# Squares turned together with T's summands, inverse norms spread by two DMAs, x's low parts on GpSimd

## The reference, cut to what matters

```python
# x: (64, 128, 512) = 64 items, 128 rows, 512 columns; adj: (128, 128); four weights of (512, 512)
def _L0_gnn_ref(x, weight, bias):            # graph over the 512 columns
    x_norm = xn / norm(xn)                   # xn = x transposed to (512, 64, 128)
    mean_sim = einsum('nbl,mbl->nm', x_norm, x_norm) / B
    A = mean_sim on its k nearest, else 0    # k = 153, then normalised by degrees -> An
    return einsum('sd,sbl->dbl', An, xn @ weight) + bias

def _L1_gnn_ref(h, causal_mask, W_lang, W_grav, W_V, W_O, gate_logit, log_sigma):   # per item, 128 rows
    z_l, z_g, v = h @ W_lang.T, h @ W_grav.T, h @ W_V.T
    zn = z_l / norm(z_l)
    A_l = maximum(zn @ zn.T, 0) * not_eye
    sq = sum(z_g * z_g, -1)
    d2 = maximum(sq + sq.T - 2 * z_g @ z_g.T, 0)
    A_g = exp(-d2 / (2 * sigma * sigma)) * not_eye
    K = w_l * row_stochastic(A_l * mask) + (1 - w_l) * row_stochastic(A_g * mask)
    return (K @ v) @ W_O.T

x = layernorm(x + _L0_gnn_ref(x, adj, bias))
x = layernorm(x + _L1_gnn_ref(x, adj, W_lang, W_grav, W_V, W_O, gate_logit, log_sigma))
```

## Time and profile before

| | us |
|---|---|
| median of 3 runs (lowest, highest) | 947.16 (945.18, 949.78) |
| the profiled execution's own time | 945.65 |
| its span, first to last instruction | 943.9 |
| PE busy in the span | 915.0 (97%) |
| DVE busy | 750.7 (80%) |
| ACT busy | 535.5 (57%) |
| POOL busy | 307.6 (33%) |

### The profile page before, as it was taken

How to read it: one execution, slowest core, us unless ns; L and a number is a source line. 1 busy time by engine, 2 the same in 40 slices (tenths; PEclk the granted TensorE clock), 3 DMA queues, 4 the chain that set the end, 5 groups by cost and what they waited for, 6 DMA issues and landing times.

```text
span 943.9 us, 18952 instructions
## 1 busy us (share of the span) xinstructions
PE 915.0 (97%) x6858; PEld 538.8 (57%) x6858; DVE 750.7 (80%) x1716; ACT 535.5 (57%) x978; POOL 307.6 (33%) x431
## 2 busy tenths in 40 slices
PE   8999998999999999999999999999999999999993
PEld 6777876565555555555555555555555555555451
DVE  5887588778787878787878787878787878786766
ACT  6887766666463736364646464646464646463531
POOL 5888272045040505050504040404040404041410
PEclk9999999999999999999999999999999999999997
DMA  7554121103232223222323232313131313121211
GB/s 306 188 200 149 54 91 45 46 1 58 89 54 94 56 89 56 88 57 87 59 86 59 85 66 79 69 76 74 71 74 71 81 63 87 59 57 46 57 45 44
DMA packets 101848, 75.84 MB, mean 80 GB/s; under 512 B 80560, under 2 KB 80688, under 8 KB 99888
## 3 DMA queue, kind: packets, MB, share of 16 engines
q1 hardware_dynamic: 101808, 75.32, 27.7%
HBM read 38.86 MB, written 16.78 MB: 59 GB/s over the span
## 4 chain that ended last, share of the span: by engine, by line
PE 62%; DVE 14%; ACT 4%; issue 3%; DMA 1%; POOL 1%; DVEq 0%; SPq 0%; ACTq 0%; POOLq 0%
PE bank L265 13%; PE bank L267 12%; PE bank L266 12%; PE pair L265 7%; PE pair L267 7%; PE pair L266 7%; DVE arena L1731 4%; DVE arena L1724 2%; DVE arena L1399 1%; PE bank L778 1%; ACT arena L1071 1%; DMA arena<-arena 1%; ACT arena L1210 1%; PE bank L753 1%; PE bank L752 1%
## 5 line engine op out<-in xcount | busy, mean ns | idle before, releaser
L265 PE MATMUL bank<-arena 128*128 128x512 f16 (+2 forms) x1056 | 292.9, 301 | 7.4 <-DMA arena<-arena 3.1
L266 PE MATMUL bank<-arena 128*128 128x512 f16 (+2 forms) x1056 | 292.4, 301 | 0.0
L267 PE MATMUL bank<-arena 128*128 128x512 f16 (+2 forms) x1056 | 292.4, 301 | 0.0
L265 PE MATMUL pair<-arena 128*128 128x512 f16 (+1 forms) x400 | 151.1, 378 | 0.0
L266 PE MATMUL pair<-arena 128*128 128x512 f16 (+1 forms) x400 | 150.6, 377 | 0.0
L267 PE MATMUL pair<-arena 128*128 128x512 f16 (+1 forms) x400 | 150.4, 377 | 0.0
L265 PEld LDWEIGHTS bank<-arena 128*128 128x128 f16 x1056 | 103.2, 98 | 68.8 <-DMA arena<-arena 4.4
L267 PEld LDWEIGHTS bank<-arena 128*128 128x128 f16 x1056 | 103.3, 98 | 63.2 <-issue 0.6
L266 PEld LDWEIGHTS bank<-arena 128*128 128x128 f16 x1056 | 103.4, 98 | 54.6 <-issue 0.3
L457 POOL TENSOR_TENSOR sq_parts<-cf,zero 128x4 bf16<-128x4 f32 x16 | 3.3, 208 | 399.2 <-DVE cf L1780 399.2
L1210 ACT ACTIVATE arena<-bank 128x512 f16<-128x512 f32 x64 | 37.6, 588 | 97.3 <-PE bank L267 97.3
(11 more groups left out here) (347 smaller groups left out, 1947.8 us busy)
## 6 DMA issues: line engine op xcount, KB each, us to landing
arena<-in_x SPq DMA_DIRECT2D x32, 1024.0 KB, 5.5
out_dram<-arena SPq DMA_DIRECT2D x15, 1024.0 KB, 4.3
arena<-arena SPq DMA_TRANSPOSE x75, 3.2
arena<-in_x SPq DMA_DIRECT2D x2, 512.0 KB, 4.6
arena<-in_w_grav_t SPq DMA_DIRECT2D x1, 1024.0 KB, 7.3
arena<-in_w_lang_t SPq DMA_DIRECT2D x1, 1024.0 KB, 5.2
arena<-in_w_v SPq DMA_DIRECT2D x1, 1024.0 KB, 8.0
arena<-in_w_o_t SPq DMA_DIRECT2D x1, 1024.0 KB, 9.0
```

What stands on the lines that cost most here:

```text
L265: pe.matmul(dst, ah, bh, start=start, stop=False)
L266: pe.matmul(dst, ah, bl, start=False, stop=False)
L267: return pe.matmul(dst, al, bh, start=False, stop=stop)
```

## The change

It has four parts.

1. Squares. TensorE's `add_turned` of gravity no longer turns the half product alone. VectorE takes the diagonal from the half product itself (`diag_g`, its sum, then `dev` = half product less its own square), ScalarE and VectorE split `dev` into high and low halves, and TensorE adds the turned `dev`. The squares along the rows come with it, so `sq_parts`, `part_rows`, `sq_rows` and `along_rows` of the squares are gone. `between(0)` now stands ahead of both `add_turned`.
2. Inverse norms. VectorE takes them from the language half product (`diag_l` before `add_turned`). SP writes them to DRAM and reads them back, spread over 128 partitions. VectorE reads them from `rn_row`. GpSimd's parts and TensorE's `part_rows` and `along_rows` of the norms are gone.
3. x. For groups 3 to 15 (in bodies 1 to 13) ScalarE writes a scaled float32 copy `x_up` beside the high part, and GpSimd subtracts; VectorE's `x_low` is gone there. ScalarE does three of the four items ahead of the first `z_high` of gravity, and the fourth behind it.
4. k_g is made by ScalarE in four instructions rather than by GpSimd in one. `k_mix` on VectorE comes ahead of the second `first_factors`.

```diff
             for g in range(1, NG):
                 store(g - 1)
+                inverses_along(g)
                 if g + 1 < NG:
                     turn_h(g + 1, (g + 1) % 2)
...
+            def inverses_along(g):
+                sp.wait_ge(s["r_ready"], g + 1)
+                sp.dma_start(rn_dram, nl[:, 5, :]).then_inc(s["rn_out"], 16)
+                sp.wait_ge(s["rn_out"], g * 16 + 16)
+                sp.dma_start(rn_row.rearrange("p b n -> p (b n)"),
+                             rn_dram.rearrange("(o n) b -> o (n b)", o=1).broadcast_to([P, N4])).then_inc(s["rn_in"], 16)
...
# GpSimd's body
+            def x_low(g, items):
+                for b in items:
+                    pool.wait_ge(s["x_up_ready"], g * GB - 3 * GB + (b + 1))
+                    pool.wait_ge(s["x_h_ready"], g * GB + (b + 1))
+                    low = pool.tensor_tensor(x_l[:, b, :], x_up[:, b, :], x_h[:, b, :], ALU.subtract)
+                low.then_inc(s["x_l_ready"], 1)
...
# TensorE's body
+                between(0)
                 pe.wait_ge(s["half_g_l_ready"], g + 1)
                 add_turned(1, s["gg_ps"])
-                between(0)
                 pe.wait_ge(s["half_l_l_ready"], g + 1)
                 add_turned(0, s["gl_ps"])
-                between(1, range(0, 1))
-                pe.wait_ge(s["sq_parted"], g + 1)
-                part_rows(0, sq_parts, s["sq_rows_ps"])
-                between(1, range(1, 3))
-                squares_along(g)
-                between(1, range(3, KB))
+                between(1)
                 between(2)
-                pe.wait_ge(s["rn_parted"], g + 1)
-                part_rows(P, rn_parts, s["rn_rows_ps"])
-                between(3, range(0, 2))
-                inverses_along(g)
-                between(3, range(2, KB))
+                between(3)
...
# ScalarE's body
+            def x_parts(g, slot, loads, b):
+                if b == 0:
+                    act.wait_ge(s[f"x_in{slot}"], loads * 16)
+                    act.wait_ge(s["x_l_ready"], g)
+                    act.wait_ge(s["xw_ps"], g * GB)
+                act.activation(x_up[:, b, :], xg[slot][:, b, :], ACT.Copy, scale=up[:, 5:6]).then_inc(s["x_up_ready"], 1)
+                act.activation(x_h[:, b, :], xg[slot][:, b, :], ACT.Copy,
+                               scale=up[:, 5:6]).then_inc(s["x_h_ready"], 1)
...
+                def k_gravity():
+                    act.wait_ge(s["cf_ready"], g + 1)
+                    wait(act, s["kT_in"], g * 16)
+                    for b in range(GB):
+                        last = act.activation(k_g[:, b, :], a_g[:, b, :], ACT.Copy, scale=cf[:, 7, b:b + 1])
+                    last.then_inc(s["kg_ready"], 1)
+
+                if has_second and has_previous:
+                    for b in range(GB - 1):
+                        x_parts(g + 2, slot, loads, b)
+                z_high(1, s["zg_ps"], s["zg_h_ready"], 0)
+                if has_second and has_previous:
+                    x_parts(g + 2, slot, loads, GB - 1)
+                for n in range(1, KB):
                     z_high(1, s["zg_ps"], s["zg_h_ready"], n)
...
# VectorE's body
-                half_low(1, s["half_g_h_ready"], s["half_g_l_ready"])
-                dve.wait_ge(s["gg_ps"], g + 1)
+                dve.wait_ge(s["half_g_ps"], g + 1)
                 dve.tensor_tensor(diag_g, gg, for_items(ident[:]), ALU.mult).then_inc(s["dg_ready"], 1)
...
+                dve.tensor_tensor(dev, gg, per_item(cf[:, 1, :]), ALU.subtract).then_inc(s["dev_ready"], 1)
...
+                dve.wait_ge(s["rn_in"], g * 16 + 16)
+                dve.tensor_tensor(a_l, gl, rn_row.rearrange("p b n -> p (b n)").rearrange("p (n b) -> p b n", b=GB),
+                                  ALU.mult).then_inc(gs, 1)
```

More of the change, by code:

```diff
@@ L235, in build @@
         tile_at = iter(range(88 * KIB, 110 * KIB, 2 * KIB))
-        diag_l, diag_g, t_l, a_l, e_g, a_g, k_g, k_mix = (
-            at(next(tile_at), [GB, P]) for _ in range(8))
+        diag_l, diag_g, dev, a_l, e_g, a_g, k_g, k_mix, rn_row = (
+            at(next(tile_at), [GB, P]) for _ in range(9))
         k_parts = at(100 * KIB, [2 * GB, P], F16)
@@ L446, in _ @@
             low(blocks(w3_l), blocks(vo_raw), blocks(w3_h), 8, s["w_l_ready"])
[L448 to L457, removed]
@@ L477, in body @@
+            def body(g, slot, has_next, has_second, has_previous):
+                if has_second and has_previous:
+                    x_low(g + 2, range(GB))
+                if has_next:
+                    for b in range(GB):
+                        residual(g + 1, 1 - slot, b)
                     for b in range(GB):
                         low_h(g + 1, 1 - slot, b)
-            body(0, 0, True)
-            with pool.Fori(0, NG // 2 - 1) as j:
+            body(0, 0, True, True, False)
@@ L482, in _ @@
+            with pool.Fori(0, NG // 2 - 2) as j:
                 for t in (1, 2):
-                    body(j * 2 + t, t % 2, True)
-            body(NG - 1, (NG - 1) % 2, False)
+                    body(j * 2 + t, t % 2, True, True, True)
+            body(NG - 3, (NG - 3) % 2, True, True, True)
+            body(NG - 2, (NG - 2) % 2, True, False, True)
+            body(NG - 1, (NG - 1) % 2, False, False, True)
         @block.tensor
@@ L768, in values @@
                     mm.then_inc(s["v_ps"], 1)
-            def part_rows(first, parts, done):
-                pe.matmul(bank[6][0:GB * PARTS, first:first + P], parts[:].rearrange("p b i -> p (b i)"), ident_b[:],
-                          start=True, stop=True).then_inc(done, 1)
-            def along_rows(dst, rows, start, done):
-                for b in range(GB):
-                    mm = pe.matmul(dst[:, b * P:(b + 1) * P], pick_item[:, b, :], rows[:], start=(start and b == 0),
-                                   stop=(b == GB - 1), skip_group_check=True)
-                mm.then_inc(done, 1)
             def weighted(g, b):
@@ L1211, in z_high, with half_high @@
                                    ACT.Copy, scale=U_DOWN).then_inc(done, 1)
-                def half_high(i, ps, done):
-                    act.wait_ge(ps, g + 1)
-                    act.activation(half_h[i], bank[4 + i][:].rearrange("p (b n) -> p b n", b=GB), ACT.Copy,
-                                   scale=HALF_DOWN).then_inc(done, 1)
+                def half_high(i, src, ready, done):
+                    act.wait_ge(ready, g + 1)
+                    act.activation(half_h[i], src, ACT.Copy, scale=HALF_DOWN).then_inc(done, 1)
                 def v_high(b):
@@ L1758, in body @@
                     xw_low(g + 1, 0)
-                if has_second and has_previous:
-                    x_low(g + 2, slot, range(0, HALF))
                 z_low(0, s["zl_h_ready"], s["zl_l_ready"], 0)
@@ L1781, in body @@
                 dve.wait_ge(s["dg_ready"], g * 2 + 2)
+                dve.tensor_tensor(dev, gg, per_item(cf[:, 1, :]), ALU.subtract).then_inc(s["dev_ready"], 1)
                 dve.tensor_scalar(cf[:, 0, :], cf[:, 1, :], c1(HK), None, ALU.mult).then_inc(s["hk_ready"], 1)
-                dve.wait_ge(s["gl_ps"], g + 1)
+                if has_second and not has_previous:
+                    x_low(g + 2, slot, range(GB))
+                dve.wait_ge(s["half_g_h_ready"], g + 1)
+                half_low(1, dev, s["half_g_l_ready"])
+                dve.wait_ge(s["half_l_h_ready"], g + 1)
                 dve.tensor_tensor(diag_l, gl, for_items(ident[:]), ALU.mult).then_inc(s["nl_steps"], 1)
+                half_low(0, gl, s["half_l_l_ready"])
                 dve.wait_ge(s["nl_steps"], g * 2 + 1)
@@ L1835, in body @@
                 if has_next:
-                    first_factors(g + 1, 1)
-                v_low(0)
+                    first_stats(g + 1, 3)
+                    first_moments(g + 1, 1)
                 dve.wait_ge(s["cl_ready"], g + 1)
@@ L1844, in body @@
                 last.then_inc(s["k_ready"], 1)
+                if has_next:
+                    first_factors(g + 1, 1)
+                v_low(0)
                 if has_next:
```

110 lines of the change are left out of this document (31 added, 79 removed).

## The result

The changed kernel took 970.28 us (median of 4 runs, 968.48 to 972.38) against 946.5 before on the same chip: ratio 1.025, 95% interval 1.0234 to 1.027, slower by 24 us. The forecast was 953.5 with 942 to 964. The direction and the wait that makes it (on x, at the start of zl) were as forecast, the size was not. The profiled execution took 969.45 us, span 967.7 against 943.9.

A forecast was written before the change was run, and what follows sets the result against it. PE was taken to bound the steady stage at 46.9 us a group; x's wait adds 0.65 in 13 groups, other groups -2: 945.65 + 8.5 - 2 = 952, or 953.5 on the medians' scale; range 942 to 964.

The forecast's parts named there:

- What is taken off PE: Spreading of squares and norms along rows: its removal saves PE 1.3 us per group, 21 us over 16 groups.
- The floor of 921: Whole kernel if PE alone decided: 45.3 us per group, 945.65 - 25 = 921 us.
- I count this pause as gone: PE's pause before the language half products, for the last `z_low`: 0.33 us lost per group, expected to vanish, 4 us.
- `dev`: Gravity's turned squares: `dev` halves ready before PE asks, so no cost; body 0 about 1.4 us late, once.
- Norms by DMA: Write and read back of inverse norms: 4.8 us at the lower end, hidden within 7.8 us, costed at nothing.
- x ahead of the first `z_high`: Start of zl: ScalarE waits for the x load, so PE idles 2 to 2.5 us in bodies 1 to 13.
- t4 + 18.6: When the next zl ends on PE: 7.0 us until x lands, 5.1 for copies and halves, 6.5 for zl, after t4.
- When is t4?: Step timing h's fourth transpose through ScalarE, VectorE and GpSimd: H + 28.65 to 29.3, giving periods of 47.25 to 47.9 us.
- t4: Start of the fourth transpose of h, behind which the x load is issued; no change in time at H + 28.4.
- H: The end of the zl products on PE, the mark from which times within a group are counted.
- The last groups: Groups outside the 13 steady ones (body 0 about even, body 14 and the last body): together -2 us.
- The rival of the falling clock: PE's clock falls after the new pause, 1.6 us lost in each of 13 groups: 974 us; chance 0.06.

The follow-up runs named there:

- `sq_only`: The kernel before with part 1 (squares by way of `dev`) alone: 942.05 us, ratio 0.9942.
- `norms_only`: The kernel before with part 2 (inverse norms by DMA) alone: 954.34 us, ratio 1.0081.
- `early_resid`: The changed kernel with the x load issued ahead of the transposes of h and `second_residual(0)` formed between VectorE's low-part multiplies: 925.78 us, ratio 0.9775.
- `load_early`: The changed kernel with only SP's order changed, the x load issued ahead of the four transposes of h: 931.02 us, ratio 0.9827.
- `x_early`: The kernel before with part 3 (x) and the x load issued ahead of the transposes of h: 942.06 us, ratio 0.9949.
- `stats_early`: The changed kernel with VectorE's `second_stats` and `second_moments` ahead of the first zg `z_low`: 966.81 us, ratio 1.018.
- `x_only`: The kernel before with part 3 (x) alone, the load still behind the transposes of h: 987.6 us, ratio 1.0417.
- `kg_short`: `kg_only` with the first two of GpSimd's four `low_h` per group cut to 32 of 512 columns: 953.06 us, ratio 1.006.
- `kg_only`: The kernel before with k_g made on ScalarE ahead of `first_norm(0)` and nothing else: 958.36 us, ratio 1.0122.
- `x_late`: The changed kernel with ScalarE's x copies back behind the four zg banks and `log_exp`, GpSimd still subtracting: 975.04 us, ratio 1.030.

## Why the prediction was wrong in size

- **"What is taken off PE"**: right, 1.3 us a group. `sq_only` and `norms_only` each bring the stage before `weighted` 0.68 earlier, and PE's own period, with the pause gone too, is 45.35 in `early_resid` where 45.3 was worked out. The floor of 921 is near its 925.8.
- **"I count this pause as gone"**: wrong in the changed kernel. 0.33 became 0.71. With x late, `z_high` is late, and with it `second_moments`, which stands behind zg's `z_low`, then `log_exp` and the zl `z_high`. With the load ahead (`load_early`, `x_early`) the pause is gone as counted; `stats_early` takes it away with the load still late.
- **`dev`**: hidden in the steady groups as said. In body 0 PE waits 0.50 and 0.74, where 1.4 had been said.
- **Norms by DMA**: hidden. The read is issued 1.45 after the write and lands 3.8 later, 5.25 for the pair, above the lower bound of 4.8 that was taken, inside 7.8. The Trainium skill ("DMA: Bandwidth & Descriptors", Anatomy of one DMA) gives its 2.0 of fixed cost for DMAs of the GpSimd path; the estimate of 4.6 for the pair that the prediction made from it is 0.65 short of the trace, which has 1.4 for 2 KB and 3.8 for 256 KB read to all partitions.
- **x ahead of the first `z_high`**: right as a mechanism, shown by `x_only`, `x_early` and `load_early`. Its term "t4 + 18.6" came out as 18.75 and 19.15 in the two groups shown, as ScalarE starts 5.8 or 6.25 after the issue, not 5.5, and as 18.6 to 18.8 in the ten others from body 2 on.
- **"When is t4?"** is the step that failed, by the pause that it counted as gone. It was given as H + 28.65 to 29.3 and measured H + 29.9. In `stats_early` and `load_early`, which have no such pause, it is H + 29.18 in every group, inside the range given; so 0.72 of the miss is the pause, which brings all of PE's marks behind it that much later. Put into the prediction's own sum, 29.18 gives 957 and 29.9 gives 966. That 29.18 lies in the range is in part luck. `k_mix`, counted as drawn out beside `low_h(1)`, ran at its usual 1.13 when `low_h(1)` was all but over. A meeting that was not counted fell earlier on the way instead: the first `first_moments` on a residual, 1.13 where such an instruction alone takes 0.21, and then ScalarE's roots behind it.

```profile
610.79 1.26 POOL L433 TENSOR_TENSOR arena<-arena 128x512 f32<-128x512 f32 x1 [1.33 <-ACT arena L1047]
...
610.95 1.13 DVE L1653 TENSOR_SCALAR ln<-mv 128x2 f32<-128x2 f32 x1
...
617.37 1.16 POOL L437 TENSOR_TENSOR arena<-arena 128x512 f16<-128x512 f32 x1 [0.25 <-ACT arena L1165]
...
618.47 1.13 DVE L1807 SCALAR_TENSOR_TENSOR arena<-arena,cf 128x128 f32<-128x128 f32 x4
```

The sum, then: t4 0.9 above the middle and the rest 0.35 make a period of 48.85 on average of the two groups where 47.55 was used; the mean of bodies 2 to 13 is 48.64. Over the 13 groups that wait for x the H marks of the two profiles give +21.0 (beside 1.25 for `dev` in body 0) against +8.5. The last groups gave back 1.0, not 2. What is left, 2.5, lies before the first H: in the profiled execution after, the clock was at half between 160 and 165 us, in that of before at full. (At one place the prediction's own sum is a little off: t4 = H + 28.0 and H + 28.7 give 941 and 950, where it has 942.5 and 952.)

```profile
160.00:165.00 5.00, 5.00 (x22) 0.50 0.51 186
```

Of the experiments' profiles `kg_short` has it whole, ten have it in part, and `load_early`, `norms_only` and `sq_only` have none of it, with the same instructions there; its cause was not found. The rival of the falling clock gave 974, near the measured time, but is not what happened in the profiled execution: every group from the first H to the last shows a clock of 1.00. In experiments with pauses of the same size it did happen (last section).

The lesson of the rows is in the order: the range held t4 from H + 28.0 to 29.7, and each 0.1 us of it is 1.3 us of time. That the parts do not add up (alone on the old kernel -5, +8, +12 and +41, together +24) is the same thing seen from outside: which chain ends last (x, h's transpose, k's transpose) changes with each edit, and VectorE's small instructions fall on GpSimd's or between them; of the 41 some 14 are the clock's.

## What to carry to other kernels

When an edit makes an engine wait for a load at the head of its row, look first where that load stands in its queue: here one issue moved ahead of a few transposes turned a loss of 24 us into a gain of 16. Where small VectorE instructions lie on a chain and GpSimd works on large tiles beside them, read the two rows side by side, and allow up to the length of GpSimd's instruction for each meeting, here 0.3 to 1.0 us. A pause that is to vanish should be followed to what feeds it in the new order before it is struck from the sum.

## What the runs showed of the hardware

*VectorE beside GpSimd.* In `kg_only` a `tensor_scalar` with one input was held as long as the instructions with two (1.08 beside 0.17). The Trainium skill ("SBUF — State Buffer", Who interferes with whom) says that two SBUF inputs, or a mode that uses both ports, which `tensor_scalar` can enter with the right operands, exclude a GpSimd instruction that reads SBUF for its whole length. By that rule the held ones would end with GpSimd's, and the trace agrees: each ends within 0.03 us of it.

*TensorE's clock after a pause.* PE coming out of a pause in `x_only`, and windows of 2 us around it (length, PE busy, count, granted clock, DMA share, GB/s):

```profile
500.74 0.39 PE L266 MATMUL bank<-arena 128*128 128x512 f16 x1 [2.25 <-DVE arena L1753]
```

```profile
497.92:499.92 2.00, 0.57 (x3) 1.00 0.00 0
499.92:501.92 2.00, 1.18 (x6) 0.99 0.00 0
501.92:503.92 2.00, 2.00 (x7) 0.50 0.00 0
503.92:505.92 2.00, 2.00 (x8) 0.66 0.00 0
505.92:507.92 2.00, 2.00 (x11) 1.00 0.00 0
```

The clock stays at full through the pause and falls to 1.2 GHz just over a microsecond after work has begun again; by the clock column 1.0 + 0.7 = 1.7 us are lost. A pause of 2.09 in the next group left it at full, and so did the 2.35 of the changed kernel. In `x_late` PE makes the same pause in each of 12 groups, 2.67 from start to start, and the clock fell behind it in four. So a pause of this size cost nearly its length again in some groups and nothing in others. In the profiled execution of `x_only` (991, the longest of its four) eight groups lost 14 us this way by the clock column, about what it lies above its sum; what decides between the two was not found.
